# Second cross-attention of a perceiver kernel: groups of four positions instead of eight, scores on column halves of the array

## The reference, cut to what matters

```python
def _L1_xattn_ref(x, context, Wq, Wkv, Wout, bout):
    q = x @ Wq
    k, v = jnp.split(context @ Wkv, 2, axis=-1)
    q, k, v = map(split_heads, (q, k, v))            # b, h, n, d
    mask = j_idx % n_q == i_idx                      # key j belongs to position j % 64
    sim = jnp.einsum('bhid,bhjd->bhij', q, k) * scale
    attn = jax.nn.softmax(jnp.where(mask, sim, max_neg), axis=-1)
    out = jnp.einsum('bhij,bhjd->bhid', attn, v)
    return merge_heads(out) @ Wout + bout
```

## Time and profile before

| | us |
|---|---|
| median of 3 runs (range) | 892.08 (889.93 to 894.46) |
| the profiled execution, its own time | 891.09 |
| its span, first to last instruction | 889.3 |
| PE busy | 838.4 (94%) |
| DVE / ACT / POOL busy | 517.6 / 421.5 / 103.8 |
| the stage from U's last copy to the last sum | 647.1 to 720.4 |

### The profile page before, as it was taken

How to read it: one execution, slowest core, us unless ns; L and a number is a source line. 1 busy time by engine, 2 the same in 40 slices (tenths; PEclk the granted TensorE clock), 3 DMA queues, 4 the chain that set the end, 5 groups by cost and what they waited for, 6 DMA issues and landing times.

```text
span 889.3 us, 20146 instructions
## 1 busy us (share of the span) xinstructions
PE 838.4 (94%) x7924; PEld 680.0 (76%) x7924; DVE 517.6 (58%) x1218; ACT 421.5 (47%) x853; POOL 103.8 (12%) x102
## 2 busy tenths in 40 slices
PE   7999999999889798999999999999989999879997
PEld 5888888888647796888888888885379957668785
DVE  6777887877537657555555555554356533675332
ACT  4666657667641224445455444443456542522221
POOL 1323331240000610000000000000011000400100
PEclk9999999999999899999999999999999999899999
DMA  8445664475180000303303303007326668033950
GB/s 319 173 144 197 232 217 168 161 261 179 48 355 1 3 4 0 140 3 141 143 0 141 141 8 134 0 0 248 130 93 240 247 252 341 13 131 117 377 235 25
DMA packets 26012, 128.15 MB, mean 144 GB/s; under 512 B 2376, under 2 KB 8416, under 8 KB 21856
## 3 DMA queue, kind: packets, MB, share of 16 engines
q1 hardware_dynamic: 24624, 110.87, 33.4%
q0 software_dynamic: 1328, 16.41, 4.7%
HBM read 126.75 MB, written 0.52 MB: 143 GB/s over the span
## 4 chain that ended last, share of the span: by engine, by line
PE 83%; DVE 9%; DMA 3%; ACT 2%; issue 2%; SPq 1%; DVEq 0%; ACTq 0%
PE PS L460 13%; PE PS L462 13%; PE PS L461 13%; PE PS L784 6%; PE PS L1229 3%; PE PS L905 3%; PE PS L796 3%; PE PS L773 3%; PE PS L1030 3%; PE PS L1241 3%; PE PS L1049 3%; PE PS L480 2%; PE PS L1018 2%; PE PS L1003 2%; DMA arena<-in_bias 2%
## 5 line engine op out<-in xcount | busy, mean ns | idle before, releaser
L1411 ACT CAST w_h<-arena 128x768 fp32r<-128x768 f32 x64 | 53.4, 835 | 124.8 <-PE PS L462 124.8
L1768 DVE TENSOR_TENSOR w_l<-arena,w_h 128x768 fp32r<-128x768 f32 x64 | 61.2, 957 | 86.7 <-ACT w_h L1411 86.6
L460 PE MATMUL PS<-xnT_h,w_h 128*128 128x512 f32 x256 | 99.7, 389 | 1.4 <-DVE xnT_l L454 1.4
L461 PE MATMUL PS<-xnT_l,w_h 128*128 128x512 f32 x256 | 99.6, 389 | 0.0
L462 PE MATMUL PS<-xnT_h,w_l 128*128 128x512 f32 x256 | 99.6, 389 | 0.0
L1613 DVE CUSTOM_DVE_ANT_0 arena<-PS,arena 128x512 f32<-128x512 f32 x128 | 86.8, 715 | 19.2 <-PE PS L773 18.0
L1309 ACT ACTIVATE arena<-arena 128x1024 f32<-128x1024 f32 x64 | 73.5, 1150 | 10.2 <-DVE arena L1613 10.1
L784 PE MATMUL PS<-consts,arena 128*128 128x128 f32 x512 | 68.3, 277 | 0.7 <-ACT arena L1314 0.4
L784 PEld LDWEIGHTS PS<-consts,arena 128*128 128x128 f32 x512 | 55.9, 141 | 10.6 <-issue 3.6
L1775 DVE TENSOR_TENSOR arena<-PS,arena 128x512 f32<-128x512 f32 x64 | 44.3, 692 | 29.4 <-PE PS L462 27.7
L460 PEld LDWEIGHTS PS<-xnT_h,w_h 128*128 128x128 f32 x256 | 48.0, 188 | 11.8 <-DVE xnT_l L454 1.8
(11 more groups left out here) (316 smaller groups left out, 1783.9 us busy)
## 6 DMA issues: line engine op xcount, KB each, us to landing
arena<-in_bias SPq DMA_DIRECT2D x64, 512.0 KB, 4.3
arena<-in_wall SPq DMA_DIRECT2D x8, 3072.0 KB, 10.0
arena<-in_wf SPq DMA_DIRECT2D x8, 2052.0 KB, 11.6
hT<-in_ctxT SPq DMA_DIRECT2D x12, 1024.0 KB, 6.0
arena<-in_ctxT SPq DMA_DIRECT2D x4, 1024.0 KB, 7.0
arena<-in_ctxG SPq DMA_DIRECT2D x4, 1024.0 KB, 5.1
hT<-in_ctxG SPq DMA_DIRECT2D x4, 1024.0 KB, 4.9
arena<-in_w SPq DMA_DIRECT2D x2, 1024.0 KB, 6.1
```

The source lines that it names most:

```text
L460: pe.matmul(out, a[0], b[0], start=start, stop=False)
L461: pe.matmul(out, a[0], b[1], start=False, stop=False)
L1411: act.copy(w_h[:, s % 4, :], stage[s // 8 % 2][:, s % 8, :]).then_inc(sem("c_wh"), 1)
L1768: dve.tensor_tensor(w_l[:, s % 4, :], stage[s // 8 % 2][:, s % 8, :], wide(w_h[:, s % 4, :]), ALU.subtract).then_inc(sem("c_wl"), 1)
```

## The change

Groups are of four positions (`QI` = 4), sixteen a batch: 4 positions x 16 heads are 64 rows, 4 positions x 16 keys are 64 columns. Two groups stand above each other, one on partitions 0 to 63, one on 64 to 127. A batch is again two halves, now of four pairs of groups.

- `sims`: per half 16 float32 matmuls with 64 output partitions and 64 columns, alternating between the two column halves of the array (32 a batch, where there were 16 of 128x128). U is kept in the order of the groups from the start (`U[dc][b*16+q, 64]`), so `Ub`, `Ub0` and the copies L661, L1805 and L1451 are gone; the copies into U (L1800, L1449) now write in runs of 4 floats, and L1072 reads its moving columns in runs of 4 floats, 256 bytes apart. The host arranges the context (`ctxD`, `ctxG`) to match.
- `scores` and `exps`: eight a batch as before, of 64 columns; `probabilities`: 256 columns a half.
- `turned`: one 128x128 transpose turns two pairs, four a batch. ACT copies the partitions 0 to 63 (L1465's place), DVE the partitions 64 to 127 (new), 256 columns each, into four blocks of `PTx`, whose other half is zero (set once by POOL).
- `sums`: 16 matmuls as before, moving two of the four blocks; the results lie in U's order, so `summed` copies contiguously.
- PE's order is new: the sims of two batches first, then eight `warm`, then per batch `sims` half 0 of batch b+1, `turned`, `sims` half 1, `sums`; four `warm` ahead of the last `turned`. All loops of the stage are unrolled. SP's two waits are for the same events as before.

PE, the middle of the loop, before. `Z` and `Ub` are printed as `arena`; `d_p`: probabilities are done, `d_te`: the turned tile is copied, `d_we`: the old sums are copied, `d_ub`: the U copies, `d_z`: the scores are read.

The diff, cut to its core:

```diff
-GRP, GI = 8, 8
+QI = 4
+QS = S // QI
+GRP = QS // 2
+GROUP_AT = ((0, 3), (2, 1))
...
-    U = cd(KC, XH, TOK)
+    U = [cd(B * QS, XH * QI) for _ in range(KC)]
...
-    Z, PTx = cd(2, 4, P), cd(2, 4, P)
+    Z, PTx = cd(2, 2, P), cd(2, 2, 4, 64)
+    zs = lambda hf, g: Z[:, hf, g // 2, (g % 2) * 64:(g % 2 + 1) * 64]
...
+            for b in range(B):
+                if b >= 2:
+                    sp.wait_ge(sem("d_sim"), 2 * (b - 1))
+                sp.dma_start(ctxT1[b % 2], A["ctxD"][b].rearrange("(k p) n -> p k n", p=P))\
+                  .then_inc(sem(f"d_ctxT{b % 2}"), 16)
+                if b >= 2:
+                    sp.wait_ge(sem("d_w"), 4 * (b - 1))
+                sp.dma_start(ctxG[b % 2], A["ctxG"][b]).then_inc(sem(f"d_ctxG{b % 2}"), 16)
...
+            def sims(b, hf):
+                pe.wait_ge(sem(f"d_ctxT{b % 2}"), b // 2 * 16 + 16)
+                if b:
+                    pe.wait_ge(sem("d_z"), 2 * (b - 1) + hf + 1)
+                for j in range(2):
+                    for at in range(2):
+                        for dc in range(KC):
+                            for n, r in enumerate(halves):
+                                q = 8 * hf + 4 * j + GROUP_AT[n][at]
+                                last = pe.matmul(PS[r, hf, (2 * j + at) * 64:(2 * j + at + 1) * 64], U[dc][:, b * QS + q, :],
+                                                 ctxT1[b % 2][:, dc, q * 64:(q + 1) * 64], start=dc == 0, stop=dc == KC - 1)
+                last.then_inc(sem("d_sim"), 1)
...
+            for b in range(2):
+                for hf in range(2):
+                    sims(b, hf)
+            warm(pe, 7, 8)
+            for b in range(B):
+                if 0 < b < B - 1:
+                    sims(b + 1, 0)
+                if b == B - 1:
+                    warm(pe, 0, 4)
+                turned(b)
+                if 0 < b < B - 1:
+                    sims(b + 1, 1)
+                sums(b)
...
-                                         U[:, ki, 2 * c + h2, :], start=ki == 0, stop=ki == KC - 1)
+                                         U[ki][:, :, QI * (2 * c + h2):QI * (2 * c + h2 + 1)], start=ki == 0, stop=ki == KC - 1)
...
-                    act.copy(U[:, 1, 2 * c + h2, :], bank(3 + 2 * h2)).then_inc(sem("d_ue1"), 1)
-            act.wait_ge(sem("d_ue0"), 2 * FC)
-            act.copy(Ub0[0].rearrange("p g (h i) -> p g h i", i=GI),
-                     U[:, 0, :, 0:S].rearrange("p h (g i) -> p g h i", i=GI)).then_inc(sem("d_ub0"), 1)
+                    act.copy(U[1][:, :, QI * (2 * c + h2):QI * (2 * c + h2 + 1)],
+                             bank(3 + 2 * h2).rearrange("p (q i) -> p q i", i=QI)).then_inc(sem("d_ue1"), 1)
...
+            def turned(b):
+                for hf in range(2):
+                    dve.wait_ge(sem("d_t"), 2 * b + hf + 1)
+                    dve.tensor_copy(PTx[S:P, hf, :, 2:4, :], PS[S:P, 2 + hf, 0:2 * P].rearrange("p (j n c) -> p j n c", j=2, n=2))\
+                       .then_inc(sem("d_te1"), 1)
...
+            for b in range(1, B):
+                scores(b, 0)
+                turned(b - 1)
+                scores(b, 1)
+                probabilities(b)
+                summed(b - 1)
+            turned(B - 1)
             summed(B - 1)
```

More of the change, by code:

```diff
@@ L46, in const_layout @@
         "half2": ((p % 32) // DK == np.arange(2)[None, :]),
-        "group": np.where(p % GI == c % GI, 0.0, -BIG),
+        "group": np.where(p % QI == np.arange(64)[None, :] % QI, 0.0, -BIG),
         "upper": i > j,
@@ L655, in _ @@
             pool.wait_ge(sem("d_ue0"), 2 * FC)
[L657 to L672, removed]
+            pool.memset(PTx.rearrange("p f g n c -> p (f g n c)"), 0.0).then_inc(sem("d_set"), 1)
+            pool.wait_ge(sem("d_w"), 4 * B)
             for n in range(2):
@@ L1019, in _ @@
                                   start=True, stop=True).then_inc(sem(f"d_u{dc}"), 1)
[L1021 to L1025, removed]
-                for hf in range(2):
[L1027 to L1034, removed]
@@ L1036, in sums @@
-            def sums(i, j):
-                b = i * 2 + j
-                for hf in range(2):
[L1039 to L1045, removed]
+            def sims(b, hf):
[10 more added lines that the diff above has]
+                last.then_inc(sem("d_sim"), 1)
@@ new lines, in turned, with sums @@
+            def turned(b):
+                for hf in range(2):
+                    pe.wait_ge(sem("d_p"), 2 * b + hf + 1)
+                    for j in range(2):
+                        last = pe.transpose(PS[:, 2 + hf, j * P:(j + 1) * P], Z[:, hf, j, :], C("ident"))
+                    last.then_inc(sem("d_t"), 1)
+            def sums(b):
+                pe.wait_ge(sem(f"d_ctxG{b % 2}"), b // 2 * 16 + 16)
+                for hf in range(2):
+                    for n in range(2):
+                        pe.wait_ge(sem(f"d_te{n}"), 2 * b + hf + 1)
@@ L1046, in sums @@
                     for dc in range(KC):
-                        pe.wait_ge(sem(f"d_we{dc}"), b * 2 + hf + 1)
+                        if b:
+                            pe.wait_ge(sem(f"d_we{dc}"), 2 * (b - 1) + hf + 1)
                         for g in range(4):
                             last = pe.matmul(PS[:, 4 + 2 * hf + dc, g * P:(g + 1) * P],
-                                             ctxG[j][:, 4 * hf + g, dc * P:(dc + 1) * P], PTx[:, hf, g, :],
+                                             ctxG[b % 2][:, 4 * hf + g, dc * P:(dc + 1) * P],
+                                             PTx[:, hf, g // 2, 1:3, :] if g % 2 else PTx[:, hf, g // 2, 0:4:3, :],
@@ L1051, in sums @@
                                              start=True, stop=True)
                         last.then_inc(sem("d_w"), 1)
[L1055 to L1063, removed]
+            for dc in range(KC):
+                pe.wait_ge(sem(f"d_ue{dc}"), 2 * FC)
+            for b in range(2):
+                for hf in range(2):
+                    sims(b, hf)
@@ L1454, in exps @@
             def exps(b):
                 for hf in range(2):
-                    act.wait_ge(sem("d_z"), b * 2 + hf + 3)
+                    act.wait_ge(sem("d_z"), 2 * b + hf + 1)
                     for g in range(4):
-                        last = act.activation(Z[:, hf, g, :], Z[:, hf, g, :], ACT.Exp, bias=mx1[:, hf, g:g + 1],
+                        last = act.activation(zs(hf, g), zs(hf, g), ACT.Exp, bias=mx1[:, hf, g:g + 1],
                                               scale=-1.0, accum_out=rs1[:, hf, g:g + 1])
@@ L1460, in exps, with turned @@
                     last.then_inc(sem("d_e"), 1)
-            def transposed(b):
+            def turned(b):
                 for hf in range(2):
-                    act.wait_ge(sem("d_t"), b * 2 + hf + 3)
-                    act.copy(PTx[:, hf].rearrange("p a b -> p (a b)"), bank(2 + hf)).then_inc(sem("d_te"), 1)
+                    act.wait_ge(sem("d_t"), 2 * b + hf + 1)
+                    act.copy(PTx[0:S, hf, :, 0:2, :], PS[0:S, 2 + hf, 0:2 * P].rearrange("p (j n c) -> p j n c", j=2, n=2))\
+                       .then_inc(sem("d_te0"), 1)
@@ L1467, in summed @@
             def summed(b):
                 for hf in range(2):
[L1469 to L1472, removed]
+                    act.wait_ge(sem("d_w"), 4 * b + 2 * hf + 2)
+                    act.copy(U[1][:, b * QS + 8 * hf:b * QS + 8 * hf + 8, :].rearrange("p q n -> p (q n)"),
+                             bank(5 + 2 * hf)).then_inc(sem("d_we1"), 1)
@@ L1474, in _ @@
             exps(0)
-            with act.Fori(1, B) as b:
-                transposed(b - 1)
+            act.wait_ge(sem("d_set"), 1)
+            for b in range(1, B):
+                turned(b - 1)
                 exps(b)
                 summed(b - 1)
-            transposed(B - 1)
+            turned(B - 1)
             summed(B - 1)
@@ L1799, in _ @@
                     dve.wait_ge(sem("d_u0"), 2 * c + h2 + 1)
[L1800 to L1819, removed]
+                    dve.tensor_copy(U[0][:, :, QI * (2 * c + h2):QI * (2 * c + h2 + 1)],
+                                    bank(2 + 2 * h2).rearrange("p (q i) -> p q i", i=QI)).then_inc(sem("d_ue0"), 1)
@@ new lines, in scores @@
+            def scores(b, hf):
+                dve.wait_ge(sem("d_sim"), 2 * b + hf + 1)
+                if b:
+                    dve.wait_ge(sem("d_t"), 2 * (b - 1) + hf + 1)
+                for g in range(4):
+                    last = dve.tensor_tensor_reduce(out=zs(hf, g), in0=PS[:, hf, g * 64:(g + 1) * 64],
+                                                    in1=C("group"), scale=-1.0, scalar=3e38, op0=ALU.add,
+                                                    op1=ALU.min, accum_out=mx1[:, hf, g:g + 1])
+                last.then_inc(sem("d_z"), 1)
@@ L1832, in summed @@
[L1832 to L1844 removed]
+                    dve.wait_ge(sem("d_w"), 4 * b + 2 * hf + 1)
@@ L1845, in _ @@
```

(15 more changed lines are left out.)

36 lines of the change are left out of this document (9 added, 27 removed).

## The result

The changed kernel takes **885.25 us** (median of 7 runs, 884.01 to 886.54) against 892.08 in the same runs; the ratio is **0.9914**, 95% interval 0.9893 to 0.9936. That is 6.8 us less, where 11.4 were forecast. Its profiled execution took 886.54 with a span of 884.7.

What follows compares the result with a forecast made beforehand. PE was taken as the bound, with context transfers binding every second batch once PE is faster: 12.85 + 42.6 + 6.45 = 61.9 us of stage against 73.3, gain 11.4, so 880.5 us; range 875.0 to 887.5.

Steps and rivals of the forecast that it cites:

- Wv's and the copies' short runs: L1072's reads and the copies into U, in runs of 4 floats: taken as free; ranges up to 13.97 and 1 us.
- L: Context transfers: time from the end of sums(k) to the earliest start of sims(k+3), forecast 7.8 us.
- W: PE's time for one steady batch of the stage: forecast 6.4 us (6.2 to 6.9), against 8.54 before.
- The beginning: From U complete to the end of the first batch's sums, filler included: forecast 12.85 us, against 15.8 before.
- the two bounds given for that: Unrolled SP queue issues ctxT some 0.3 us sooner; its landing was said to come 0 to 0.3 sooner.
- The last batch: End of the stage: four warm, transposes, a wait and the sums, forecast 6.45 us.
- rival 4: Stage with longer transfers and stalls: L 9.1, W 6.6, stalls 2; gain 4.9 us, 886.2 us; chance 0.08.
- The clock: PE idling about 1.4 us in every second batch was said to leave its clock at 1.00, no cost.
- Instruction stops: Unrolled PE code might stop without named cause, as L1229 does for 0.34 us: range 0 to 2.5, taken 0.

Runs made afterwards that it cites:

- e1: Changed kernel with all 16 sims instructions of one column half, then all 16 of the other, instead of alternating; 890.09 us, ratio 0.9976.
- e8: Changed kernel with the edits of e1 and e2 together: sims one column half at a time, context issued ahead; 888.43 us, ratio 0.9955.
- e2: Changed kernel with the next batch's scores context issued ahead of this batch's sums context in the SP queue; 879.24 us, ratio 0.9869.
- e6: Kernel before the change with the context transfers ordered as in e2 and SP's loop unrolled; 891.91 us, ratio 0.9996.
- e3: Changed kernel without its twelve filler matmuls (eight ahead of the first transposes, four ahead of the last); 879.50 us, ratio 0.9869.
- e7: Changed kernel with e2's transfer order, three filler matmuls first and none last, DVE's turned-tile copies ahead of the next scores; 872.03 us, ratio 0.9764.
- e5: The changed kernel itself, unedited, measured and profiled a second time; 884.31 us, ratio 0.9901.

## Why the prediction was right, and what was mis-sized

**The mechanism** held in each step: the halves overlap (e1, e8), the transfers bind every second batch (e2), they hardly did before (e6), the filler is longer than the wait it fills (e3), Wv's and the copies' short runs cost nothing. The time lies in the range, and the gain is 6.8 us for 11.4. By the terms of the sum 12.85 + 3 (L + W) + 6.45 = 61.9, measured 65.3 in the stage:

- *The beginning*: 13.6 (650.21 to 663.81) for 12.85. Four sims 4.36 for 4.1, and 0.1 until they start; the filler 3.65 for 3.5; the sums 3.82 for 3.6. From the filler's end to the sums it is 1.67, as forecast.
- *W*: 6.86 for 6.4. The sims half was right (1.08 for 1.05, its change of shape included); the term most off is the sums, 3.57 and 0.08 for a change. I took the start-to-start time of the matmuls as if the next batch followed almost without a seam, but the row of the kernel before said 3.81, and 3.82 it was. The transposes took 0.58 for 0.52, the first sims behind a transfer 1.15. The wait for DVE's copy was 0.23 for 0.1 (the chain calls it "issue"; it is gone in e7, where the copy comes first). Even in e7, where nothing waits, a batch is 6.52 for the forecast's 6.25: with the rates of the sum for the rest, the four changes of shape cost 0.57 and not 0.3.
- *L*: 8.55, 7.35 and 8.74 (from the end of the sums to the start of the sims) for 7.8; in e5 9.0, 7.5 and 8.7. I took the median of five pairs of the kernel before, and these are not the pairs of the changed one. Before, the five ctxT landed 6.3 to 7.6 after their issue (median 6.6); now 6.9 to 8.3 (median 8.1), each behind a ctxG of the same size, and issued 0.38 us behind it instead of 0.7 or more. So issuing sooner brought nothing, and of the two bounds given for that zero was right. The third and seventh batch were the late ones of the chain in all five profiles without e2's edit, the fifth came early; why, no run here tells.
- *The last batch*: 6.49 for 6.45.

W and L enter threefold: 1.4 + 1.2 of the 3.4 us that the stage lacks, 0.75 the beginning. The 65.3 lie midway between the forecast's 61.9 and rival 4's 68.4, and by the mechanism of rival 4, longer transfers and a longer W, without its stops. The other 1.2 between the stage's 8.0 and the median's 6.8 lie outside the stage; the repeated run gave 8.3 (892.65 to 884.31), and runs of one kernel differ by several us, so that remainder is not told from scatter.

**The clock** was wrong as a rule, not as a size. I argued from one row that PE may idle 2.10 us at 1.00, and put the cost at nothing. e5 and e6 lost the clock after waits of 2.21 and 2.10, e3 after two shorter ones; the first profile of the changed kernel did not after 1.77, so there the zero was right by luck. The price, 1.3 to 1.6 us each time (e3's sums 5.44 for 3.82, e6's sims 5.45 for 3.83, e5's batch 8.12 for 6.86), belongs in the range of every wait that the forecast makes.

**Instruction stops** as those of the earlier trace rows did not appear in the unrolled stage, where every wait of PE in the timeline has a named cause: nought was right.

## What to carry to other kernels

When an engine that bounds a loop gets faster, first look up which event releases each transfer of the loop and what stands ahead of it in its queue: here a prefetch two batches deep was in truth one batch deep, since it stood behind a transfer with a later event, and moving it forward was worth 4.7 us of the stage, where the whole change had brought 8.0. Price an edit that removes work where nothing else binds and where it does: the overlap was worth 9.6 us of the stage in the one and 6.7 in the other. Filler work that is to keep a clock should not be much longer than the wait it fills; measure it by leaving it out and read the granted clock behind the wait.

## What the runs showed of the hardware that was not expected

The granted clock after a wait of PE is not settled by the length of the wait alone: 2.10 us of idling left it at 1.00 in the kernel before and were followed by a 7 us window at 0.76 at the same place in e6; 1.77 left it at 1.00 in the changed kernel, while 2.21 were followed by a 4 us window at 0.65 in the same kernel's second profile; and behind two waits of 0.89 and 0.69 it was 0.67 in e3. What decides is not shown.

Float32 matmuls of 128 rows on alternating column halves start every 0.031 us at 64 columns with different moving columns in the two halves (64 of them from 650.31 to 652.31 in the first profile), hardly slower than the 0.030 of the earlier trace rows, where both move the same; 32 of them between matmuls of the whole array come to 0.034 each, against 0.057 on one half at a time.

A transfer of 1 MB issued 0.38 us behind another lands 6.9 to 8.3 us after its issue in the first profile of the changed kernel, the first of the pair 4.6 to 4.9.
